# Graph attention and GRU graph convolution on one core: a new order of VectorE and TensorE work in layer 0, the statistics of batch b+2 later, its normalized h in one piece

## The reference

```
h = relu(layernorm(x))
Wh = h @ W;  e = leaky(Wh@a1 [rows] + Wh@a2 [columns]);  e = -9e15 where adj == 0
x = x + elu(softmax(e) @ Wh)                       # attention
h = relu(layernorm(x))
for l in 0, 1, 2:                                  # GRU over the graph
    g = A^T (h W_l);  A = (adj != 0)
    r, z = sigmoid(g@w_ih_{r,z} + h@w_hh_{r,z} + b)
    n = tanh(g@w_ih_n + b + r * (h@w_hh_n + b))
    h = (1 - z) * n + z * h
x = x + h
```

## Time and profile before

| | |
|---|---|
| median of 3 runs | 689.55 us |
| the profiled execution | 689.75 us, span 687.9 us, granted clock 0.984 |
| PE busy | 623.6 us, 91% of the span |
| DVE busy | 539.0 us, 78% |
| ACT busy | 451.9 us, 66% |
| POOL busy | 255.4 us, 37% |
| a full body (b = 1 to 5) | 80.4 us |

### The profile page before, as it was taken

The page is one execution under the profiler, slowest core; times in us unless marked ns, Lnnn a source line. Parts: engine busy times, 40 slices in busy tenths (PEclk is TensorE's granted clock), DMA queues, the critical chain, the costliest instruction groups (busy, mean ns, idle before and its releaser), DMA issues.

```text
span 687.9 us, 8791 instructions
## 1 busy us (share of the span) xinstructions
PE 623.6 (91%) x2845; PEld 458.4 (67%) x2845; DVE 539.0 (78%) x1234; ACT 451.9 (66%) x777; POOL 255.4 (37%) x263
## 2 busy tenths in 40 slices
PE   2686999998999899998999989998999999999995
PEld 2465776676686676776766766766767776767774
DVE  4767998599876998779985998769987699648545
ACT  2784787477874778566875778647785677554443
POOL 1203544246241461525432453414715234413440
PEclk9799899999999999999999999999999999999998
DMA  6521131023202132022410132021320122001001
GB/s 222 183 93 62 62 121 32 33 61 123 92 31 92 33 123 92 15 79 61 146 39 32 62 123 92 30 81 44 122 93 6 56 87 67 1 1 30 1 1 30
DMA packets 28669, 47.39 MB, mean 69 GB/s; under 512 B 1672, under 2 KB 19408, under 8 KB 28624
## 3 DMA queue, kind: packets, MB, share of 16 engines
q1 hardware_dynamic: 28624, 46.84, 21.0%
HBM read 42.60 MB, written 4.23 MB: 68 GB/s over the span
## 4 chain that ended last, share of the span: by engine, by line
PE 55%; DVE 26%; ACT 8%; issue 5%; POOL 5%; DMA 1%; DVEq 0%; ACTq 0%; POOLq 0%
PE ps_x L970 14%; PE ps_g L1008 10%; PE ps_x L951 6%; DVE score L665 5%; DVE zh L757 3%; ACT score L389 3%; PE ps_r L1017 2%; DVE zh L764 2%; PE ps_z L1018 2%; PE ps_z L1017 2%; PE ps_r L1019 2%; PE ps_r L1018 2%; PE ps_z L1019 2%; DVE hkT L751 2%; DVE nn L744 2%
## 5 line engine op out<-in xcount | busy, mean ns | idle before, releaser
L1008 PE MATMUL ps_g<-edges,h_hi 128*128 128x512 f32 x384 | 157.7, 411 | 10.6 <-DVE h_lo L773 9.2
L1008 PE MATMUL ps_g<-edges,h_lo 128*128 128x512 f32 x384 | 152.2, 396 | 0.0
L389 ACT ACTIVATE score<-score,nmax 128x1024 f32<-128x1024 f32 x64 | 73.8, 1153 | 48.1 <-DVE nmax L665 47.1
L970 PE MATMUL ps_x<-probT,h_nat 128*128 128x512 f32 x224 | 98.9, 594 | 0.0
L1008 PEld LDWEIGHTS ps_g<-edges,h_hi 128*128 128x128 f32 x384 | 73.1, 190 | 29.0 <-DVE h_lo L773 12.8
L665 DVE CUSTOM_DVE_ANT_0 score<-score,away 128x1024 f32<-128x1024 f32 x64 | 86.6, 1353 | 7.3 <-ACT score L383 6.5
L300 POOL TENSOR_SCALAR tz<-tz 128x512 f32<-128x512 f32 x32 | 24.6, 769 | 172.9 <-ACT tz L430 172.9
L275 POOL TENSOR_SCALAR rstd<-mv 128x4 f32<-128x4 f32 (+1 forms) x24 | 9.9, 412 | 199.4 <-DVE mv L707 146.9
L1008 PEld LDWEIGHTS ps_g<-edges,h_lo 128*128 128x128 f32 x384 | 73.2, 191 | 14.0
L396 ACT ACTIVATE probT<-ps_x 128x512 f32<-128x512 f32 x128 | 70.9, 595 | 17.2 <-PE ps_x L951 17.1
L951 PE MATMUL ps_x<-ident,score 128*128 128x128 f32 x512 | 71.0, 281 | 11.4 <-ACT score L389 10.0
(11 more groups left out here) (136 smaller groups left out, 1331.5 us busy)
## 6 DMA issues: line engine op xcount, KB each, us to landing
adj_in<-in_adj SPq DMA_DIRECT2D x64, 512.0 KB, 3.3
x_nat<-in_x SPq DMA_DIRECT2D x8, 512.0 KB, 4.3
ej<-ej_kept_at SPq DMA_DIRECT2D x8, 512.0 KB, 3.4
out<-nn SPq DMA_DIRECT2D x16, 256.0 KB, 2.3
probT<-in_L_gnn_weight SPq DMA_DIRECT2D x1, 192.0 KB
probT<-in_L_gnn_w_ih SPq DMA_DIRECT2D x1, 192.0 KB
probT<-in_L_gnn_w_hh SPq DMA_DIRECT2D x1, 192.0 KB
ej_kept_at<-ej_row SPq DMA_DIRECT2D x8, 4.0 KB
```

The source lines that it names most:

```text
L389: act.activation(score[t % U][:], score[t % U][:], ACT.Exp, bias=nmax[:, t:t + 1], scale=-1.0, accum_out=rowsum[:, t:t + 1]).then_inc(exp_ ...
L970: last = pe.matmul(bank_of("agg", c, par)[:], h_nat[par][:, j, :], probT[:, j, :], start=(j == 0), stop=(j == T - 1))
L1008: last = pe.matmul(ps_g[c][:], part[:, s, :], edges[par][:, s, cols(c)], start=(s == 0 and part is h_hi), stop=(s == T - 1 and part is h_lo))
```

## The change

Five things are reordered; no instruction is added or removed in a full body.

1. VectorE, layer 0: g_lo of the first half stands between the two out halves, g_lo of the second behind scores 1. `away` tile 1 of batch b+2 is made at the end of body b, behind tile 0. n_input(b, 0, 0) comes before away 2 and scores 2; the edges tiles come later. n_input of half 1 is split in `r_times_hn` and `add_in`, with `lo_half(b, 0, 0)` between them.
2. The statistics `norm1(b + 2)` move from behind scores 1 to behind scores 4, ahead of g_lo of layer 1. GpSimd's `rstd1` moves to the start of its layer 1 part.
3. ScalarE writes h_nat of batch b+2 in one piece behind leaky tile 6 instead of in two.
4. TensorE: tile 0's transposes come ahead of the second h_back of the batch before. In layer 0, half 0, z of h is computed ahead of r of h; hn waits for the first out half alone, and r for the second.
5. TensorE: h_back(b, 0, 0) moves ahead of the product into ps_in of half 1, and in `early_neighbours` half of the second group of neighbours goes ahead of the h_back.

```diff
@@ -324,9 +324,9 @@
                 split_h(0, 0, 1)
 
             def body(b, par, attend, prepare):
-                if prepare:
-                    rstd1(b + 2)
                 for l in range(L - 1):
+                    if prepare and l == 1:
+                        rstd1(b + 2)
                     z_times_h(b, l, 0)
                     z_times_h(b, l, 1)
                     split_h(b, l + 1, 0)
@@ -505,8 +505,6 @@
                 hi_half(b, 0, 1)
                 if attend:
                     leaky_tile(a, a_par, 4)
-                if prepare:
-                    h_tiles(b + 2, par, 0)
                 if attend:
                     exp_tile(a, 3)
                 g_hi_half(b, 1, 0)
@@ -524,6 +522,7 @@
                 if attend:
                     leaky_tile(a, a_par, 6)
                 if prepare:
+                    h_tiles(b + 2, par, 0)
                     h_tiles(b + 2, par, 1)
                 if attend:
                     exp_tile(a, 6)
@@ -724,10 +723,18 @@
                 dve.tensor_tensor(g_lo[c][:], ps_g[c][:], g_hi[c][:], ALU.subtract).then_inc(g_lo_done, 1)
 
             def n_input(b, l, c):
+                r_times_hn(b, l, c)
+                add_in(b, l, c)
+
+            def r_times_hn(b, l, c):
 
                 n = b * QS + 2 * l + c + 1
                 dve.wait_ge(tr_done, n)
                 dve.scalar_tensor_tensor(pre[c][:], tr[c][:], 1.0, hnb[c][:], ALU.add, ALU.mult).then_inc(rh_done, 1)
+
+            def add_in(b, l, c):
+
+                n = b * QS + 2 * l + c + 1
                 dve.wait_ge(rh_done, n)
                 dve.wait_ge(in_ps, n)
                 dve.tensor_tensor(pre[c][:], pre[c][:], ps_in[:], ALU.add).then_inc(pre_done, 1)
@@ -802,6 +809,7 @@
                 setup_layer(2)
                 split_h0(0, 1, True)
                 away_tile(1, 1, 0)
+                away_tile(1, 1, 1)
 
             def body(b, par, attend, prepare):
                 a, a_par = b + 1, 1 - par
@@ -810,39 +818,38 @@
                     scores(a, 0)
                 else:
                     out_half(b - 1, a_par, 0)
-                if attend:
-                    away_tile(a, a_par, 1)
+                g_lo_half(b, 0, 0)
                 if b > 0:
                     out_half(b - 1, a_par, 1)
                 if attend:
                     scores(a, 1)
-                if prepare:
-                    norm1(b + 2, par)
-                g_lo_half(b, 0, 0)
                 g_lo_half(b, 0, 1)
-                if attend:
-                    edge_tile(a, a_par, 0)
+                n_input(b, 0, 0)
+                if attend:
                     away_tile(a, a_par, 2)
                     scores(a, 2)
-                n_input(b, 0, 0)
+                new_h(b, 0, 0)
+                if attend:
+                    edge_tile(a, a_par, 0)
+                r_times_hn(b, 0, 1)
+                lo_half(b, 0, 0)
+                add_in(b, 0, 1)
                 if attend:
                     edge_tile(a, a_par, 1)
-                new_h(b, 0, 0)
-                if attend:
+                new_h(b, 0, 1)
+                if attend:
+                    away_tile(a, a_par, 3)
                     edge_tile(a, a_par, 2)
-                n_input(b, 0, 1)
-                lo_half(b, 0, 0)
-                new_h(b, 0, 1)
-                if attend:
-                    away_tile(a, a_par, 3)
 
                 lo_half(b, 0, 1)
                 if attend:
+                    scores(a, 3)
                     edge_tile(a, a_par, 3)
-                    scores(a, 3)
                     away_tile(a, a_par, 4)
                     edge_tile(a, a_par, 4)
                     scores(a, 4)
+                if prepare:
+                    norm1(b + 2, par)
                 g_lo_half(b, 1, 0)
                 g_lo_half(b, 1, 1)
                 if attend:
@@ -880,6 +887,7 @@
                     split_h0(a, 0)
                 if prepare:
                     away_tile(b + 2, par, 0)
+                    away_tile(b + 2, par, 1)
                 if attend:
                     att_half(a, a_par, 1)
                     x1_half(a, a_par, 1)
@@ -1028,8 +1036,8 @@
             def hn_of_h(b, l, c):
 
                 n = b * QS + 2 * l + c + 1
-                if l == 0 and c == 0:
-                    pe.wait_ge(out_done, b * 2 + 1)
+                if l == 0 and c == 0 and b > 0:
+                    pe.wait_ge(out_done, b * 2)
                 h = part_of_h(b, l, c)
                 if c == 1:
                     pe.wait_ge(hnb_done, n - 1)
@@ -1041,10 +1049,15 @@
                 h = part_of_h(b, l, c)
                 if c == 1:
                     pe.wait_ge(tr_done, n - 1)
+                if l == 0 and c == 0:
+                    product(ps_z[:], whh(1), h, True, False)
+                    if b > 0:
+                        pe.wait_ge(out_done, b * 2 + 1)
                 product(ps_r[:], whh(0), h, True, False)
                 if c == 1:
                     pe.wait_ge(tz_done, n - 1)
-                product(ps_z[:], whh(1), h, True, False)
+                if l > 0 or c == 1:
+                    product(ps_z[:], whh(1), h, True, False)
 
             def gates_h(b, l, c):
                 hn_of_h(b, l, c)
@@ -1069,6 +1082,8 @@
                 pe.wait_ge(g_lo_done, n)
                 product(ps_r[:], of_g(0), g, False, True).then_inc(r_ps, 1)
                 product(ps_z[:], of_g(1), g, False, True).then_inc(z_ps, 1)
+                if l == 0 and c == 1:
+                    h_back(b, 0, 0)
                 if c == 1:
                     pe.wait_ge(pre_done, n - 1)
                 product(ps_in[:], of_g(2), g, True, True).then_inc(in_ps, 1)
@@ -1103,8 +1118,9 @@
                 def early_neighbours(l):
 
                     neighbours(b, par, l, 0, 0)
+                    neighbours(b, par, l, 0, 1, range(0, TH // 2))
                     h_back(b, l - 1, 1)
-                    neighbours(b, par, l, 0, 1)
+                    neighbours(b, par, l, 0, 1, range(TH // 2, TH))
 
                 def late_neighbours(l):
                     neighbours(b, par, l, 1, 0)
@@ -1115,17 +1131,16 @@
                 if b > 0:
                     h_back(b - 1, 2, 0)
                 neighbours(b, par, 0, 1, 1)
+                if attend:
+                    probT_tile(a, a_par, 0)
                 if b > 0:
                     h_back(b - 1, 2, 1)
-                if attend:
-                    probT_tile(a, a_par, 0)
                 gates_h(b, 0, 0)
                 gates_g(b, 0, 0)
                 if attend:
                     probT_tile(a, a_par, 1)
                 gates_h(b, 0, 1)
                 gates_g(b, 0, 1)
-                h_back(b, 0, 0)
                 if attend:
                     probT_tile(a, a_par, 2)
```

More of the change, by code:

```diff
@@ L818, in body @@
                     scores(a, 1)
-                if prepare:
-                    norm1(b + 2, par)
-                g_lo_half(b, 0, 0)
                 g_lo_half(b, 0, 1)
+                n_input(b, 0, 0)
+                if attend:
+                    away_tile(a, a_par, 2)
+                    scores(a, 2)
+                new_h(b, 0, 0)
                 if attend:
                     edge_tile(a, a_par, 0)
-                    away_tile(a, a_par, 2)
-                    scores(a, 2)
-                n_input(b, 0, 0)
+                r_times_hn(b, 0, 1)
+                lo_half(b, 0, 0)
+                add_in(b, 0, 1)
                 if attend:
                     edge_tile(a, a_par, 1)
-                new_h(b, 0, 0)
-                if attend:
-                    edge_tile(a, a_par, 2)
-                n_input(b, 0, 1)
-                lo_half(b, 0, 0)
                 new_h(b, 0, 1)
@@ L837, in body @@
                     away_tile(a, a_par, 3)
+                    edge_tile(a, a_par, 2)
                 lo_half(b, 0, 1)
                 if attend:
+                    scores(a, 3)
                     edge_tile(a, a_par, 3)
-                    scores(a, 3)
                     away_tile(a, a_par, 4)
```

## The result

| kernel | median us (runs) | ratio to before, 95% interval | body 2 to 3, us | T - S | clock |
|---|---|---|---|---|---|
| before | 689.5 (4) | | 80.39 | 11.45 | 0.984 |
| changed | 716.84 (715.69 to 717.29, 4) | 1.0395 [1.0377, 1.0413] | 83.43 | 12.32 | 0.967 |

The change makes the kernel 27.3 us slower. S is the start of scores(a, 1), T the end of h of layer 0, half 0, as in the prediction. Between the two profiled executions the span grew from 687.9 to 713.9 us, by 26.0. "Body 2 to 3" is S to the next S. S to S over bodies 1 to 5 is 83.6 us on average, against 80.4.

The account below looks back on a forecast made before the run. The prediction took TensorE, busy 76.08 of 80.40 us in a full body, to bound the kernel. 689.75 us plus 21.0 for the bodies and 4.2 for the clock gave 715.0 us, range 697 to 723.

Parts of the forecast that it names:

- The sum: Whole kernel: 2.8 us in each of bodies 0 to 5, body 6 4.8, body 7 -0.6, clock 4.2; +25.2 us.
- The waits that go: TensorE, start of layer 0: 1.25 us of waiting filled with transposes, r of g earlier; gains nothing by itself.
- Where T goes: Layer 0, half 0: away 2, scores 2, exp 2 precede tanh of n; T = S + 12.41, 0.96 us later.
- TensorE until T: TensorE's matmuls end at S + 8.6 at the latest, then it waits 3.8 us at h_back(b, 0, 0).
- After T: Rest of layer 0 into layer 1: h of half 1 and g_lo later, +1.85 us a body (bounds 0.85, 2.4).
- The clock: TensorE's clock falls around T in most bodies; about 0.6 us a body, seven bodies, 4.2 us.
- The rest of the sum: All terms without the clock: bodies 0 to 5 16.8, body 6 4.8, body 7 -0.6; +21.0 us, 710.8.
- Rival 1: TensorE's clock stays up, all else as forecast: 711 us; chance 0.22.
- Rival 3: If exp 2 does not delay tanh of n (scores 2 through by S + 6.8): faster, 681.6 us; chance 0.07.

Follow-up runs that it names:

- the wait filled: Changed kernel with 15 more matmuls in TensorE's wait ahead of h_back(b, 0, 0), in bodies 0 to 6: 715.10 us.
- the statistics alone: Kernel before with only norm1 moved behind scores 4, rstd1 moved to layer 1 and h_nat in one piece: 682.77 us, ratio 0.9908.
- the run with both orders: Changed kernel, but scores 2 ahead of n_input, layer 0's second half in the old order, both scores ahead of g_lo in body 0: 683.32 us.
- scores 2 early: Changed kernel with away 2 and scores 2 back ahead of n_input of half 0: 688.32 us, ratio 0.9989.

## Why the prediction was right

The forecast was 715.0 us and the measured median is 716.84. The sum has +25.2 us; the medians differ by 27.3, the profiled spans by 26.0. By its steps:

- *The waits that go.* Right. Three waits of 3.1 us in all became 0.38, and the body did not get shorter by it.
- *Where T goes.* Forecast S + 12.41, measured S + 12.32; tanh of r handed over at S + 4.65 (4.66), scores 2 through at S + 8.90 (8.94), exp 2 at S + 8.95 (8.98). GpSimd's hold is shown by the run in which it waits (T back to S + 11.35). That the order of scores 2 is the cause is shown by the run that moves it.
- *TensorE until T.* Forecast 3.8 us of wait, measured 4.12.
- *After T.* The last h_lo ended at T + 8.74 (8.9), r of g of layer 1 began at T + 16.19 against T0 + 14.09 before: +2.10, where the sum has 1.85. The h of half 1 came at T + 6.5 and not T + 5.8. Its second step ran while GpSimd was at its split (1.67 us); neither the place of the product ahead of it nor the clock has a part in it, as two runs show.
- *The clock.* It fell as forecast, in bodies 0 to 6. Its price was mis-sized: 4.2 us in the sum, 0.8 us at most in the profiled spans (713.9 and 713.1) and 1.7 in the medians with the wait filled. The sum charged 0.6 us in each of seven bodies; the profiled executions show 0.1 to 0.3 in three of them and under 0.1 in the other four.
- *The rest of the sum* was too low. With the wait filled and the clock up, the span is 25.2 us above the kernel before, where the sum without the clock has 21.0: 4.2 us too little, against 3.4 too much for the clock.
- *Body 0* was not priced by itself. Up to S of body 1 the loss is 5.3 us, against 3.4 in the sum with the clock. The sum lets body 0 gain from the statistics' move as a full body does, and it does not: in the kernel before TensorE has no wait for g_lo there, and the statistics alone leave S of body 1 where it was (155.04, 155.01), while full bodies gain 1.3 us each. A g_lo that waits for its g_hi now stands between scores(1, 0) and scores(1, 1):

```profile
76.25 0.69 DVE L723 TENSOR_TENSOR g_lo<-ps_g,g_hi 128x512 fp32r<-128x512 f32 x1 [1.85 <-ACT g_hi L416]
76.86 1.22 DVE L664 CUSTOM_DVE_ANT_0 score<-score,away 128x1024 f32<-128x1024 f32 x1
```

S of body 0 moved from 73.08 to 76.86, but little of that counts. The run with both orders has the two scores ahead of g_lo in body 0 and its S there at 74.35; S of body 1 is at 156.10 all the same, against 156.31 with scores 2 early.

The parts by place: to S of body 1 +5.3 (3.4), bodies 1 to 5 +16.0 (17.0), from S of body 6 to the end +4.7 (4.8); in all 26.0 us of span against 25.2. The last part hides two misses: up to the first out half of body 7 it is +4.6 (5.4), and body 7 itself, forecast 0.6 us shorter, is 0.15 longer; there the h of half 1 came at T + 5.98 instead of T + 4.46. That the clock's price and the terms that were too small offset each other is luck; the total is nearer than its parts. What carries the forecast is the chain to T, which came out to 0.1 us.

Rival 1 had the clock's small price about right for the wrong reason: the clock fell and cost little. Rival 3's first half was true, as the statistics alone show (forecast 681.6, measured 682.8); its condition was not met in the changed kernel.

## What to carry to other kernels

When an operation is moved behind a wait on one engine, look for who consumes its result on another engine, and what stands behind that consumer in its list: here scores 2 delayed exp 2, and tanh of n was queued behind exp 2, so 1.8 us of VectorE work in the wrong place (2.8 with GpSimd's hold) cost 3.8 us of T in every body (S + 12.32 against S + 8.55). Waits that vanish on the busiest engine are worth nothing until the next thing it needs comes earlier; write down when that comes before counting them. And judge the parts of a bundled change one at a time: one part of this one gains 6.6 us.

## What the runs showed of the hardware

- A wait added to GpSimd made the program 7.0 us faster. The scores tile on VectorE (two SBUF inputs) and GpSimd's product on SBUF held each other up: 2.20 us when they met and 1.23 when they did not for the same scores tile, 1.83 and 1.26 us for the product in the same pair of runs.
- The granted clock fell to 0.50 around waits of 4.12 us, at the same place of every body but not at the same moment: in body 2 it read 0.88 from 255.00 to 257.00, where TensorE took up work at 256.26; in body 1 it read 0.80 from 170.00 to 172.00, where TensorE was idle until 172.69. It cost the program 1 to 2 us in 715, although matmuls ran at half rate in seven bodies: in four of them a chain on VectorE, not TensorE, set when the next wait ended, and in the three with the longer slow stretch 0.1 to 0.3 us each was left.
